# Experts' loop by pairs of blocks, with the last 48 inner columns of a pair as two column tiles of 64

## The reference

```python
probs = softmax(x @ gate_w.T)                    # 1024 tokens x 64 experts
topk_w, topk_idx = top_k(probs, 6)               # six experts for each token
h = silu(einsum('th,eih->tei', x, experts_w1))   # 256 channels -> 176 inner columns
y = einsum('tei,ehi->teh', h, experts_w2)        # 176 -> 256
routed_out = einsum('teh,te->th', y, combine)    # weighted sum over the six
out = routed_out + shared_out
x = x + layernorm(out)
```

## Time and profile before

| | |
|---|---|
| median of 3 runs | 311.77 us (310.48 to 313.64) |
| the profiled execution | 310.85 us, span 309.1 us |
| PE busy | 256.3 us (83%) |
| DVE, ACT, POOL busy | 176.4, 106.6, 129.5 us |
| moved by DMA | 76.07 MB, mean 246 GB/s |

### The profile page before, as it was taken

One profiled execution on the slowest core, in us unless ns is written; L12 is line 12 of the kernel. 1 busy time (PEld: TensorE's weight loads), 2 busy tenths in 40 slices (PEclk: granted clock), 3 DMA queues, 4 the chain that ended last, 5 costly groups with the idle time before them and its releaser, 6 DMA issues.

```text
span 309.1 us, 4502 instructions
## 1 busy us (share of the span) xinstructions
PE 256.3 (83%) x1361; PEld 202.0 (65%) x1361; DVE 176.4 (57%) x599; ACT 106.6 (34%) x255; POOL 129.5 (42%) x166
## 2 busy tenths in 40 slices
PE   6749959391965499919889999999999999999990
PEld 6324848260434354807778999999999999963780
DVE  4349887899797348002557777444444444448184
ACT  2484551298015601241212222224444442220032
POOL 6009300005676635676565545444444455550000
PEclk9997989768796579987999999999999999999998
DMA  6999999991222293244799999744999951189613
GB/s 237 351 341 342 338 383 386 422 406 72 89 105 90 95 372 142 90 140 145 217 378 413 325 344 409 296 141 147 301 306 341 332 182 62 65 287 382 235 34 103
DMA packets 40857, 76.07 MB, mean 246 GB/s; under 512 B 4672, under 2 KB 30848, under 8 KB 40320
## 3 DMA queue, kind: packets, MB, share of 16 engines
q1 hardware_dynamic: 35264, 60.35, 57.3%
q0 software_dynamic: 5568, 15.42, 13.2%
HBM read 44.08 MB, written 31.67 MB: 245 GB/s over the span
## 4 chain that ended last, share of the span: by engine, by line
PE 38%; issue 24%; DVE 18%; DMA 11%; ACT 5%; POOL 1%; SPq 1%; ACTq 0%; POOLq 0%; DVEq 0%
DMA x_slots<-rows,slot_i 7%; PE bank L864 6%; PE bank L871 5%; PE bank L861 5%; PE bank L872 5%; PE bank L697 5%; DVE stats L973 3%; DMA rows<-y_rows 3%; PE bank L705 3%; PE bank L879 3%; DVE xT L1275 2%; PE bank L911 2%; PE bank L938 1%; DVE rows L1022 1%; ACT rows L590 1%
## 5 line engine op out<-in xcount | busy, mean ns | idle before, releaser
L525 POOL DMA_INDIRECT y_rows<-zbuf,token_i x66 | 64.0, 970 | 63.5 <-DVE zbuf L1284 61.7
L499 POOL DMA_INDIRECT x_slots<-rows,slot_i x48 | 47.1, 981 | 63.0 <-issue 41.7
L1284 DVE COPY zbuf<-bank 128x256 f32<-128x256 f32 x66 | 28.0, 425 | 66.2 <-issue 32.1
L654 ACT ACTIVATE hT<-bank 128x128 f32<-128x128 f32 x66 | 18.3, 277 | 97.0 <-issue 63.1
L1275 DVE COPY xT<-bank 128x256 f32<-128x256 f32 x66 | 27.4, 416 | 17.1 <-PE bank L879 12.6
L745 PE MATMUL bank<-x2nT,sgu_sb 128*128 128x512 f32 (+1 forms) x48 | 27.7, 726 | 10.3 <-DVE nt L1226 6.4
L879 PE MATMUL bank<-ident,early 128*128 128x128 f32 x128 | 25.6, 281 | 7.8 <-DMA early<-x_slots 7.8
L871 PE MATMUL bank<-w_sb,hT 128*128 128x256 f32 x96 | 28.9, 383 | 2.0 <-ACT hT_r L655 2.0
L861 PE MATMUL bank<-xT,w_sb 128*128 128x128 f32 x192 | 30.1, 280 | 0.0
L864 PE MATMUL bank<-xT,w_sb 128*112 128x128 f32 x192 | 29.3, 276 | 0.0
L872 PE MATMUL bank<-w_sb,hT_r 112*128 112x256 f32 x96 | 28.7, 379 | 0.0
(11 more groups left out here) (204 smaller groups left out, 448.6 us busy)
## 6 DMA issues: line engine op xcount, KB each, us to landing
w_sb<-pairs SPq DMA_DIRECT2D x24, 752.0 KB
x_slots<-hidT SPq DMA_DIRECT2D x8, 1056.0 KB, 13.4
early<-x_slots SPq DMA_DIRECT2D x64, 132.0 KB
y_rows<-zeros SPq DMA_DIRECT2D x6, 1024.0 KB, 10.9
rows<-pairs SPq DMA_DIRECT2D x8, 752.0 KB, 6.3
rows<-y_rows SPq DMA_DIRECT2D x4, 1024.0 KB, 8.8
rows<-y_rows SPq DMA_DIRECT2D x4, 512.0 KB, 5.8
y_rows<-zbuf,token_i POOLq DMA_INDIRECT x66
```

What stands on the lines that cost most here:

```text
L499: pool.indirect_dma_start(x_slots, bass.IndirectOffsetOnAxis(ap=slot_i[:, c, k:k + 1], axis=0), xrow[c // TB][:, c % TB, k, :], None).then ...
L525: pool.indirect_dma_start(y_rows, bass.IndirectOffsetOnAxis(ap=token_i[:, s % 16:s % 16 + 1].bitcast(U32), axis=0), yS[:, s % 8, :], None) ...
L1284: dve.tensor_copy(yS[:, s % 8, :], y_b[s % 2][:, 0:C]).then_inc(y_done, 1)
```

## The change

All loops over blocks go over 33 pairs `t` (`NP`) instead of 66 blocks:

- PE: step `t` is `turn_rows(t+1)`, `hidden(t)`, `output(t-1)`, each for both blocks of the pair. It waits for the rows of both. The four transposes go to one bank. The last 48 columns of each block are products of 48 weight columns, into output partitions 0 to 47 for the even block and 64 to 111 for the odd one, in the order (k=0, even), (k=0, odd), (k=1, even), (k=1, odd).
- ACT: one silu of 128x256 and two of 48x128 a pair, in place of two of 128x128 and two of 48x128.
- DVE: one copy of 128x512 to `xT` and one of the token numbers a pair; the output copies stay two, now from four banks instead of two (banks 4 and 6 are new, so PE first waits for the shared expert's copies `dn_cp`, and after the loop for all output copies).
- SP and POOL: the same DMAs in the same order; their waits on `token_done` and `y_ps` count pairs.

```diff
-            def hidden(s):
-                u, w = s % 2, weights(s)
-                for k in range(KC):
-                    pe.matmul(h_b[u][:, 0:P], w[:, PK * k + P * u:PK * k + P * u + P], xT[:, u, k, :],
-                              start=(k == 0), stop=(k == KC - 1))
-                for k in range(KC):
-                    mm = pe.matmul(h_b[u][0:HALF + IR, P:2 * P], w[:, PK * k + 2 * P:PK * k + PK], xT[:, u, k, :],
-                                   start=(k == 0), stop=(k == KC - 1))
+            def hidden(t):
+                u, w = t % 2, weights(2 * t)
+                for i in range(2):
+                    for k in range(KC):
+                        pe.matmul(h_b[u][:, P * i:P * i + P], w[:, PK * k + P * i:PK * k + P * i + P], xT[:, u, i, k, :],
+                                  start=(k == 0), stop=(k == KC - 1))
+                for k in range(KC):
+                    for i in range(2):
+                        at = PK * k + 2 * P + HALF * i
+                        mm = pe.matmul(h_b[u][HALF * i:HALF * i + IR, 2 * P:3 * P], w[:, at:at + IR], xT[:, u, i, k, :],
+                                       start=(k == 0), stop=(k == KC - 1))
                 mm.then_inc(h_ps, 1)
...
+            def output(t):
+                u, w = t % 2, weights(2 * t)
+                for i in range(2):
+                    y = y_b[2 * u + i][:, 0:C]
+                    pe.matmul(y, hT[:, u, P * i:P * i + P], w[:, PW2 + C * i:PW2 + C * i + C], start=True, stop=False)
+                    mm = pe.matmul(y, hT_r[0:HALF + IR, 2 * u + i, :], w[0:HALF + IR, PW2 + 2 * C:PW], start=False, stop=True)
+                mm.then_inc(y_ps, 1)
...
             for s in range(E - 8):
-                sp.wait_ge(token_done, s + 1)
+                sp.wait_ge(token_done, s // 2 + 1)
                 load_rows(s + 8)
...
                 if s % 2 and 4 * RING <= s < 6 * RING:
-                    sp.wait_ge(y_ps, s + 1)
+                    sp.wait_ge(y_ps, (s + 1) // 2)
                     load_pair(s // 2 + RING)
...
+            for t in range(-1, NP + 1):
+                if t + 1 < NP:
+                    for s in (2 * t + 2, 2 * t + 3):
+                        ...
+                            pe.wait_ge(xg_in[expert(s) % 8], 16 * (expert(s) // 8 + 1))
+                    turn_rows(t + 1)
+                if 0 <= t < NP:
+                    hidden(t)
+                if t >= 1:
+                    output(t - 1)
```

More of the change, by code:

```diff
@@ L39, in moe_block @@
     NB = E + EXTRA
+    NP = NB // 2
     X0 = E - 8
@@ L42, in moe_block @@
     YTRASH = TOPK * NTOK
+    assert EXTRA == 2 and X0 % 2 == 0
     assert NT == 8 and KC == 2 and B == 2 and E % 2 == 0 and 0 < IR <= HALF and len(SC) == 3
@@ new lines, in output, with turn_rows @@
+            def output(t):
+                u, w = t % 2, weights(2 * t)
+                for i in range(2):
+                    y = y_b[2 * u + i][:, 0:C]
+                    pe.matmul(y, hT[:, u, P * i:P * i + P], w[:, PW2 + C * i:PW2 + C * i + C], start=True, stop=False)
+                    mm = pe.matmul(y, hT_r[0:HALF + IR, 2 * u + i, :], w[0:HALF + IR, PW2 + 2 * C:PW], start=False, stop=True)
+                mm.then_inc(y_ps, 1)
+            def turn_rows(t):
+                for i in range(2):
+                    s = 2 * t + i
+                    src = xz[:, s - X0, :] if is_extra(s) else xg[:, expert(s) % 8, :]
+                    for k in range(KC):
+                        at = C * i + P * k
+                        mm = pe.transpose(x_b[t % 2][:, at:at + P], src[:, P * k:P * k + P], ident[:])
@@ L883, in _ @@
             pe.wait_ge(count_read, 1)
[L884 to L894 removed]
+            pe.wait_ge(dn_cp, 4)
+            for t in range(-1, NP + 1):
+                if t + 1 < NP:
+                    for s in (2 * t + 2, 2 * t + 3):
+                        if is_extra(s):
+                            pe.wait_ge(xz_in[s - X0], 16)
+                        else:
+                            pe.wait_ge(xg_in[expert(s) % 8], 16 * (expert(s) // 8 + 1))
+                    if t >= 1:
+                        pe.wait_ge(xT_done, t)
+                    turn_rows(t + 1)
+                if 0 <= t < NP:
+                    if is_extra(2 * t):
                         pe.wait_ge(w_ext[0], 64)
@@ L897, in _ @@
                     else:
-                        pe.wait_ge(w_ld[home(expert(s) // 2)], loaded(expert(s) // 2))
-                    pe.wait_ge(xT_done, s + 1)
-                    if s >= 2:
-                        pe.wait_ge(h_done, 2 * s - 2)
-                    hidden(s)
-                if s >= 1:
-                    pe.wait_ge(h_done, 2 * s)
-                    if s >= 3:
-                        pe.wait_ge(y_done, s - 2)
-                    output(s - 1)
+                        pe.wait_ge(w_ld[home(expert(2 * t) // 2)], loaded(expert(2 * t) // 2))
+                    pe.wait_ge(xT_done, t + 1)
+                    if t >= 2:
+                        pe.wait_ge(h_done, 3 * t - 3)
+                    hidden(t)
+                if t >= 1:
+                    pe.wait_ge(h_done, 3 * t)
+                    if t >= 3:
+                        pe.wait_ge(y_done, 2 * t - 4)
+                    output(t - 1)
             def add_rows(k, c, rows):
@@ L912, in add_rows @@
                                  stop=(k == 0 and c == 1))
-            pe.wait_ge(h_done, 2 * NB)
+            pe.wait_ge(h_done, 3 * NP)
             for _ in range(KEEP):
@@ L930, in _ @@
                         pe.wait_ge(o_y, NT * e + c + 1)
-                        pe.matmul(y_b[0][:, 0:C], hT[:, 0, :], ow12[:, KC * I:KC * I + C], start=True, stop=False)
+                        pe.matmul(y_b[0][:, 0:C], hT[:, 0, 0:P], ow12[:, KC * I:KC * I + C], start=True, stop=False)
                         pe.matmul(y_b[0][:, 0:C], hT_r[0:IR, 0, :], ow2b, start=False, stop=True).then_inc(o_y_ps, 1)
             pe.wait_ge(diag_done, LOW * NT)
-            pe.wait_ge(xT_done, NB)
+            pe.wait_ge(xT_done, NP)
+            pe.wait_ge(y_done, NB)
             pe.wait_ge(ya_in[LOW], 16)
```

106 lines of the change are left out of this document (47 added, 59 removed).

## The result

Four runs took 321.2 to 326.48 us, median 323.0, against 312.5 for before (four runs). The ratio is 1.032, 95% interval 1.024 to 1.041: slower, by some 10.5 us, inside the range and on the side I gave most weight, but more than twice the +4.4 that I forecast. The profiled execution was the longest of the four (326.48 us, span 324.7), 3.5 over the median, so I compare stretches and not totals, and the same stretches in other kernels further down. Ratios are of executions within 1.5% of the fastest of their kernel, which leaves this one out.

What follows compares the result with a forecast made beforehand. PE's stream of products was taken to bound the loop. PE's loop end 1.9 us later (with stall 1.5, clock 1.0, DMA 1.0) plus 2.5 at the end gave +4.4 on 311.8: 316.2 us, range 304 to 329.

Steps and rivals of the forecast that it cites:

- PE's stream bounds the loop: Loop over blocks: nothing between PE's products waits, so a microsecond of PE work saved is one of time.
- The pair, 3.81: PE's step for two blocks in the loop: 3.94 - 0.88 + 0.55 + 0.20 = 3.81 us.
- slots: A pair's eight narrow instructions: partial overlap of two tiles in five slots of 0.11, 0.55 us in place of 0.88.
- The changes of tile: Two switches of column tile a pair on PE: 0.10 us each, 0.20 a pair; upper end 0.27 each.
- The fill, 4.6 us: Loop start: hidden values of 2 blocks, 3 outputs and a turn move behind block 5's rows, 4.6 us.
- The clock, 1.0 us: Loop start: PE newly idles, so the first two pairs may run at the lower clock level; 1.0 us taken.
- The stall near 161, 1.5 us: Loop near 161 us: ACT sees PE's product late, as in the kernel before; 1.5 us kept.
- DMA, 1.0 us from the shrunken lead: Blocks 33 to 47: rows behind SP's wait for an output have 7.6 us of lead, before 11.3; 1.0 us stall.
- The end, 2.5 us: Behind PE's last output: later scatters and loads of `y_rows` make the tail 1 to 4 us later; 2.5 taken.
- Free changes: Rival for the loop: tiles overlap and changing them costs nothing, pair 3.50 us, 306.3 us in all; chance 0.22.
- no overlap: Rival for the loop: tiles don't overlap, pair 4.14 us, 326.8 us in all; chance 0.28, shared with full changes.
- DMA as the pace: Rival where weights are loaded: eight pairs at DMA's 4.1 us, 3.50 elsewhere, 309.2 us in all; chance 0.08.

Runs made afterwards that it cites:

- e2: The changed kernel with the narrow products of both blocks in one and the same column tile; 329.72 us, ratio 1.065 to before.
- e1: The changed kernel with the last 48 columns again as padded products of 112 weight columns in one tile; 321.63 us, ratio 1.033 to before.
- e12_lead: The changed kernel with the waited-for weight pairs one pair later in SP's queue, so rows go out ahead of that wait; 319.44 us, ratio 1.037 to before.
- e3_k_inner: The changed kernel with a pair's four narrow products ordered even k=0, even k=1, odd k=0, odd k=1; 321.11 us, ratio 1.033 to before.
- e4: The changed kernel with the turns of the second and third pair put behind the products of the pair ahead; 319.0 us, ratio 1.024 to before.
- e5: The changed kernel with SP's loads for the two extra blocks at block 24 of its queue, not 12; 319.96 us, ratio 1.028 to before.
- e6: The changed kernel with 15 in place of 10 products that only keep PE going behind the loop; 319.22 us, ratio 1.024 to before.
- e8_all: The changed kernel with the edits of e4, e5, e6 and e12_lead, a count per output, and output(30) ahead of hidden(31); 312.91 us, ratio 1.008 to before.

## Why the prediction was right or wrong

The change was slower, as forecast, and the time lies in the range. But the sum had +4.4 us and the medians +10.5, and two of its terms came near by luck, as said below.

- *PE's stream bounds the loop.* Right: where nothing waits the pair follows the sum of its products and of the changes of tile in all kernels, 3.67 to 4.27. (A slip beside it: DVE is busy in 42 to 72% of the four stretches of the earlier trace rows, not 48 to 72, and POOL in 48 to 73%. Nothing in the sum hangs on it.)
- *The pair, 3.81.* Measured 3.84, but as the sum of two terms of which each was off. Overlap: I took 0.55 for the eight, by slots; e2 and the change show half of 0.88, 0.44. The changes of tile: I took 0.20 a pair, from the restart's 0.10; e1 and e2 show 0.33. The errors, -0.11 and +0.13, cancel, and that is luck. The upper end that I gave for a change, 0.27, holds; it costs 0.165. The Trainium skill, TensorEngine Tiling (Array Packing), Key Properties, has a change of mode drain the engine: the trace agrees that a change costs PE time, and 0.165 us is the price here; it doesn't show whether a drain is the reason. The Trainium skill's TensorE: Matmul & The Clock Gate, Part 3, has 2.38 for three column tiles, and my estimate for two from it was 1.6; the two tiles here give the full factor of two.
- *The fill, 4.6 us.* Right in kind and size: by the forecast the fourth pair's turn stands 9.4 us behind the turn of block 3 (2 x 2.8 for the rows of block 5 and a pair of 3.81), and it is 9.32 in e12_lead and 9.35 in e3_k_inner, where the clock costs nothing. The later turns of e4 get back 2.4 of it.
- *The clock, 1.0 us.* Right in kind, and its size is luck: in the third pair it costs 2.8 us in the change's profile, but 0.0 in e2, e3 and e12 and 1.4 to 1.8 in e1, e5 and e6, which have the same order there, 1.1 in the mean of the seven. I had not looked for it at two other places: behind the idle time near 187 (1.6 us more, from 188.15 to 193.58 for one pair) and at the end.
- *The stall near 161, 1.5 us, kept from before.* Not there. The change loses 0.4 us to a late engine, near 174.
- *DMA, 1.0 us from the shrunken lead.* Right in place (e12 removes it) and about right in size: 1.4 us of idle time in the change's profile, 0.3 in e1 and 3.2 in e3.
- *SP and the extra blocks.* Missing from the sum. I took SP's order as unchanged and so at no cost. But what it waits for there hangs on POOL's fourth scatter, and this on the first outputs, which the fill delays: the scatter starts at 164.90, before at 152.96 (161.23 in e3, 160.81 in e12). Over two pairs this cost 3.6 us, 2.0 of it in the wait and 1.6 by the clock; in e1, e3, e4, e6 and e12 it cost 1.8 to 3.9, in e2 with its slower pairs nothing, and nothing in e5.
- *The end, 2.5 us.* Mis-sized: 5.5 in the profiled execution, 2.2 to 7.0 over the kernels with the same end, 4.8 in the mean of seven (the change, e1 to e5 and e12). The first load's start (1.9 ahead of PE's end; I said 1.8) and the last scatter (2.8 behind; 2.9) were right. The third load was used at 12.9, not 11.6; in the mean of the seven it comes 3.3 us later than before. The rest are the ten instructions at the low clock, which I had not priced: 1.7 us here, 1.5 in the mean.
- The sum for the profiled execution: A's part from the third turn, 132.9 against 124.9 before, +8.0 (forecast +1.9). Of the 6.1 between them the two pairs behind SP's wait are 3.6, the clock at the start 1.8, the pair 1.0 and the rows near 240 another 0.8, less 1.1 for the stall that wasn't there. B +5.5 (forecast 2.5). Ahead of them +2.2, in which the kernel's own part can't be told from the scatter of arrivals (the same turn starts at 147.3 to 151.9 in e1 to e6 and e12).
- *The rivals.* Free changes and no overlap both fall by e1 and e2. DMA as the pace falls by e12.

## What to carry to other kernels

Two column tiles of 64 give the full factor of two on narrow float32 products, but each way in and out has a price of about one and a half instruction distances: put as many narrow products as possible between two changes, and compare the price with what they save (here 0.43 against 0.33 a pair). A coarser loop step is not free in a stream that looks PE-bound: price the first step against the arrival of its last input, the last step against what its outputs start, and every wait of the DMA queue whose condition is now met a step later. Where an engine newly idles, allow for the slow clock behind it: it came in some executions and not in others at the same place (0.0 to 2.8 us). And when a mend makes data come earlier, look again at the filler work that was sized for the later time: the 15 products of e8_all outlast the wait that they were to fill.

## What was unexpected of the hardware

- The order of products over the two tiles makes no difference (3.84 us a pair both ways), though each product's two instructions go to one tile.
- A change costs 0.165 us of PE: 0.33 for two a pair, and a group with two changes for two pairs takes 7.34 where single pairs take 7.68. Part of it stands in the trace as a weight load of the first product in the other tile that nothing hides.
- ACT and DVE sometimes take PE's result late, near the loop's start and near 175 us, behind waits that the profile ends by "remote": 5.9 us of idle time ahead of ACT's silu at 175.72 in the change, 6.0 ahead of DVE's copy at 148.05 in e8_all, and in before 3.2 and 2.0 ahead of DVE's output copies at 148.54 and 162.29. PE loses less by them, 0.4 us at the first place. Their cause stays open.
- What the low clock costs at one place differs between executions of nearly the same kernel: 6.67 us for the third pair in the change, 5.73 in e1_padded, 3.86 in e12_lead.
